# Column attention's row sums: four column tiles at once, in two runs of four products, each behind one half's scores of a later group

## The reference, cut to what matters

```python
scores = jnp.einsum('neax,nebx->neab', Q * scale, K)      # each sequence as 16 heads x 256 x 8
A = jax.nn.softmax(scores, axis=2)                        # over a, not over b
Out = jnp.einsum('neab,neax->neax', A, V)                 # V weighted by the row sums of A
```

## Time and profile before

| what | value |
|---|---|
| median of 3 executions | 1783.86 us (1780.13 to 1784.83) |
| the profiled execution, its own time | 1789.27 us |
| its span in the profile | 1787.5 us |
| PE busy | 1688.6 us (94%) |
| DVE busy | 1340.3 us (75%) |
| ACT busy | 1307.9 us (73%) |
| POOL busy | 1124.5 us (63%) |
| loop of the column attention | from 847.7 us to 1106.9 us of the span |

### The profile page before, as it was taken

The page is one execution under the profiler, slowest core; times in us unless marked ns, Lnnn a source line. Parts: engine busy times, 40 slices in busy tenths (PEclk is TensorE's granted clock), DMA queues, the critical chain, the costliest instruction groups (busy, mean ns, idle before and its releaser), DMA issues. The chain is left out here.

```text
span 1787.5 us, 43489 instructions
## 1 busy us (share of the span) xinstructions
PE 1688.6 (94%) x15560; PEld 1096.2 (61%) x15560; DVE 1340.3 (75%) x2367; ACT 1307.9 (73%) x4472; POOL 1124.5 (63%) x1014
## 2 busy tenths in 40 slices
PE   8997899999989999998999999899999999999999
PEld 5663677775657777554344444477776556777655
DVE  5554898974778989456688886698985688898645
ACT  5444788887358888745899998688887537888863
POOL 6554899992579999603212220799996278999730
PEclk9999999999999999999799999999999999999999
DMA  2002111103011110202655551211102102110111
GB/s 69 2 2 62 25 32 25 26 20 86 13 41 29 29 26 20 63 1 40 125 93 107 87 95 34 68 28 31 26 19 55 51 1 55 26 31 20 43 30 42
DMA packets 67309, 74.90 MB, mean 42 GB/s; under 512 B 13380, under 2 KB 50968, under 8 KB 65048
## 3 DMA queue, kind: packets, MB, share of 16 engines
q1 hardware_dynamic: 67096, 72.13, 18.9%
HBM read 28.08 MB, written 10.49 MB: 22 GB/s over the span
## 5 line engine op out<-in xcount | busy, mean ns | idle before, releaser
L457 POOL TENSOR_TENSOR rsum<-pa,pb 128x512 f32<-128x512 f32 x256 | 325.7, 1294 | 67.1 <-DVE pa L373 37.7
L839 ACT ACTIVATE ffn_prob<-sc,ffn_nmax 128x128 f32<-128x128 f32 x928 | 327.5, 387 | 6.8 <-DVE ffn_nmax L756 6.8
L923 POOL TENSOR_TENSOR ffn_prob<-ffn_prob,ffn_rden 128x512 f32<-128x512 f32 x256 | 265.7, 1060 | 54.3 <-DVE ffn_rden L771 46.7
L466 POOL TENSOR_TENSOR rsum<-rsum,ffn_rnt 128x512 f32<-128x512 f32 x256 | 262.0, 1045 | 8.2 <-ACT ffn_rnt L861 5.9
L383 DVE TENSOR_TENSOR pb<-proj,ffn_tab 128x512 f32<-128x512 f32 x236 | 161.5, 685 | 84.4 <-ACT rn L427 84.1
L839 ACT ACTIVATION_READ_ACCUMULATOR ffn_prob<-sc,ffn_nmax 128x1 f32 x928 | 209.5, 226 | 0.0
L363 PE MATMUL pt<-ident,rsum 128*128 128x128 f32 x960 | 154.2, 284 | 15.1 <-POOL rsum L466 12.4
L756 DVE TENSOR_REDUCE ffn_nmax<-sc 128x4 f32<-128x512 f32 x232 | 148.5, 682 | 16.1 <-PE sc L653 13.4
L363 PEld LDWEIGHTS pt<-ident,rsum 128*128 128x128 f32 x960 | 100.8, 141 | 96.6 <-ACT ffn_ptb L847 70.5
L394 DVE TENSOR_REDUCE ffn_ss<-rn 128x16 f32<-128x1024 f32 x128 | 154.4, 1206 | 0.0
L682 PE MATMUL ob<-ffn_ptb,ffn_v 128*64 128x64 f32 (+1 forms) x3072 | 143.7, 243 | 9.1 <-issue 9.1
(11 more groups left out here) (291 smaller groups left out, 4275.7 us busy)
## 6 DMA issues: line engine op xcount, KB each, us to landing
ffn_v<-ffn_v SPq DMA_DIRECT2D x128, 128.0 KB, 2.3
column_ks<-qk_parts SPq DMA_DIRECT2D x64, 128.0 KB, 4.1
rn<-Y SPq DMA_DIRECT2D x32, 128.0 KB, 2.3
qk_parts<-column_hi SPq DMA_DIRECT2D x64, 64.0 KB, 1.6
qk_parts<-column_lo SPq DMA_DIRECT2D x64, 64.0 KB, 1.7
column_qs<-qk_parts SPq DMA_DIRECT2D x32, 128.0 KB
column_qs<-qk_parts SPq DMA_DIRECT2D x64, 64.0 KB
rn<-Y SPq DMA_DIRECT2D x32, 127.5 KB, 2.4
```

The costliest lines, as they stand in the source:

```text
L457: pool.tensor_tensor(K.sm[:, r, w], K.m1[:, r, w], K.m2[:, r, w], ALU.add).then_inc(S.f_sum, 1)
L466: pool.tensor_tensor(heads(K.sm[:, r, w]), heads(K.sm[:, r, w]), K.rnt[:, r, w * HEADS:(w + 1) * HEADS].unsqueeze(2).broadcast_to([P, HEAD ...
L839: ins = act.activation(K.prob[:, r, e, k], score_banks(i)[e][:, tokens(k)], ACT.Exp, bias=K.nmax[:, r, e, k:k + 1], accum_out=K.den[:, r, ...
L923: pool.tensor_tensor(K.prob[:, r, e], K.prob[:, r, e], K.rden[:, r, e].unsqueeze(2).broadcast_to([P, 4, P]), ALU.mult).then_inc(S.f_pn, 1)
```

## The change

In the column attention PE's `row_sums` takes as its last argument bt in place of the half: one run has four products for the four tiles c = 0 to 3 with the same bt. A run with bt = 0 stands behind `scores(., 1)` of the next group, the one with bt = 1 behind `scores(., 0)` of the group after that. All waits on b_rs and b_rd count whole groups now. The product of a projection moves ahead of `scores(., 1)`. The finish of a sequence moves back: take, widen, weigh on DVE to groups 1, 2, 3 of the next sequence and residual to group 0 of the one after it; turn and spread on PE to groups 2 and 3, project to group 0 of the sequence after. After the loop PE has one more run of row sums and a `project` ahead of the last two runs, DVE a `residual`. In the local attention two of ACT's copies change places at tiles 27 and 28.

```diff
 (local attention, ACT)
-            if 1 <= i <= LATE:
+            if 1 <= i <= LATE + 1:
                 keep_probabilities(i - 1)
             if 0 <= i < TILES:
                 exponentials(i)
             if LATE + 1 < i < TILES:
                 keep_output(i - 2)
-            if LATE < i <= TILES:
+            if LATE + 1 < i <= TILES:
                 keep_probabilities(i - 1)
...
-            if 1 <= i <= LATE:
+            if 1 <= i < LATE:
                 keep_output(i - 1)
             if 0 <= j - 1 < TILES:
                 keep_queries(act, K, n, j - 1, pt[0])
+            if i == LATE:
+                keep_output(i - 1)
 (column attention, PE)
-            def row_sums(q, G, h):
+            def row_sums(q, G, bt):
...
-                pe.wait_ge(S.b_rd, 8 * q + 2 * G + h + 1)
+                pe.wait_ge(S.b_rd, 8 * q + 2 * G + 2)
...
-                for bt in range(2):
-                    for c in B_HALVES[h]:
-                        mm = pe.matmul(row_banks[q % 2][32 * c:32 * c + 4, 0:SEQ], B.rd[:, G, c, bt], B.E[:, 4 * (G % 2) + c, bt],
-                                       start=(G == 0 and bt == 0), stop=(G == 3 and bt == 1))
+                for c in range(4):
+                    mm = pe.matmul(row_banks[q % 2][32 * c:32 * c + 4, 0:SEQ], B.rd[:, G, c, bt], B.E[:, 4 * (G % 2) + c, bt],
+                                   start=(G == 0 and bt == 0), stop=(G == 3 and bt == 1))
...
-                    before = (q, G - 1) if G else (q - 1, 3)
+                    step = 4 * q + G
                     scores(q, G, 0)
-                    if before[0] >= 0:
-                        row_sums(*before, 0)
-                    scores(q, G, 1)
+                    if step >= 2:
+                        row_sums(*divmod(step - 2, 4), 1)
                     g = (q + 3) // 2
                     if 1 <= g < PAIRS:
                         if q % 2 and G <= 1:
                             product(g, G)
                         if q % 2 == 0 and G == 0:
                             product(g, 2)
-                    if q >= 1 and G >= 1:
-                        (turn, spread, project)[G - 1](q - 1)
-                    if before[0] >= 0:
-                        row_sums(*before, 1)
+                    scores(q, G, 1)
+                    if step >= 1:
+                        row_sums(*divmod(step - 1, 4), 0)
+                    if q >= 2 and G == 0:
+                        project(q - 2)
+                    if q >= 1 and G >= 2:
+                        (turn, spread)[G - 2](q - 1)
+            row_sums(SEQS - 1, 2, 1)
+            project(SEQS - 2)
             row_sums(SEQS - 1, 3, 0)
 (column attention, DVE)
-                    dve.wait_ge(S.b_rs, 8 * (q - 1) + 2 * G + h + 1)
+                    dve.wait_ge(S.b_rs, 8 * (q - 1) + 2 * G + 2)
...
-                    if q >= 1:
-                        (take, widen, weigh, residual)[G](q - 1)
+                    if q >= 2 and G == 0:
+                        residual(q - 2)
+                    if q >= 1 and G >= 1:
+                        (take, widen, weigh)[G - 1](q - 1)
...
+            residual(SEQS - 2)
             take(SEQS - 1)
 (column attention, ACT)
-                                act.wait_ge(S.b_rs, 8 * q + 2 * G + h - 3)
+                                act.wait_ge(S.b_rs, 8 * q + 2 * G - 2)
```

More of the change, by code:

```diff
@@ L1776, in scores @@
                     mm.then_inc(S.b_sc, 1)
-            def row_sums(q, G, h):
-                if q == 0 and G == 0 and h == 0:
+            def row_sums(q, G, bt):
+                if q == 0 and G == 0 and bt == 0:
                     pe.wait_ge(S.b_zero, 2)
-                pe.wait_ge(S.b_rd, 8 * q + 2 * G + h + 1)
-                if G == 0 and h == 0 and q >= 2:
+                pe.wait_ge(S.b_rd, 8 * q + 2 * G + 2)
+                if G == 0 and bt == 0 and q >= 2:
                     pe.wait_ge(S.b_rc, q - 1)
-                for bt in range(2):
-                    for c in B_HALVES[h]:
-                        mm = pe.matmul(row_banks[q % 2][32 * c:32 * c + 4, 0:SEQ], B.rd[:, G, c, bt], B.E[:, 4 * (G % 2) + c, bt],
-                                       start=(G == 0 and bt == 0), stop=(G == 3 and bt == 1))
+                for c in range(4):
+                    mm = pe.matmul(row_banks[q % 2][32 * c:32 * c + 4, 0:SEQ], B.rd[:, G, c, bt], B.E[:, 4 * (G % 2) + c, bt],
+                                   start=(G == 0 and bt == 0), stop=(G == 3 and bt == 1))
                 mm.then_inc(S.b_rs, 1)
```

## The result

The changed kernel takes 1801.99 us (median of 4, 1798.28 to 1808.2) against 1782.17 us of the kernel before (4 runs, 1780.13 to 1784.83): a ratio of 1.0114, 95% interval 1.0094 to 1.0135. It is slower, by 1.1%, where 1766 us was forecast. The range, 1757 to 1776, does not hold it, and the way it went had a chance of 0.04.

The account below looks back on a forecast made before the run. ACT was taken to bound the column attention, with gaps in it; savings of 11.8 + 1.2 + 2.7 + 2.0 - 0.1 = 17.6 us against the median of 1783.86 gave 1766 us, range 1757 to 1776.

Parts of the forecast that it names:

- the clock rival: Column attention: thinner PE work lowers the clock to 1.2 GHz and makes the kernel slower; 1810 with ten such sequences; chance 0.04.
- The rival's price: Column attention at 1.2 GHz: some 4.4 us more per sequence than forecast; 1810 with ten low sequences; chance 0.04.
- The run of row sums: PE in the column attention: a run of four products takes 0.53 us instead of 0.97.
- Group 0: Column attention, sequences 2 to 12: a gap of 0.4 us ahead of the next group's exponentials instead of 0.78.
- Group 1: Column attention, odd sequences: a gap of 0.25 us, with `take` in place of `residual`.
- Groups 2 and 3: Column attention, no projection there: both gaps (0.51 and its like in odd sequences) go, with 0.1 to spare.
- `take`: DVE in the column attention: `take` runs without idle time before it, where it had waited 0.82 us.
- `weigh`: DVE in group 3: needs `spread`, about 5.95, takes 0.33; maximum at 6.4, exponential at 7.1 us.
- Sequence 1: Column attention's low-clock stretch: groups 0 and 1 take 10.8 us instead of 13.49, 2.7 us saved.
- The local attention: Copy swaps at tiles 27 and 28, four times: PE's scores come 0.47 us earlier, 2.0 us saved (0 to 4).
- The new wait on a row sum: Rival: exponentials wait for a just-issued run; half of 56 groups lose 0.3, 8 us back, 1774; chance 0.16.

Follow-up runs that it names:

- the kernel with `project` first: Changed kernel with `project` ahead of the second scores, projection behind them, four-tile runs only in some groups from sequence 2 on: 1766.65 us, 0.9917 to the kernel before.
- the old order with wide runs: Kernel before with both row-sum runs four column tiles wide, one behind the other: 1809.69 us, ratio 1.0148.
- the kernel with the early two tiles: Changed kernel with two-tile row-sum runs in sequences 0 and 1 only, no added work: 1804.63 us, 1.0105 to the kernel before.
- full filler, start in two tiles: Changed kernel plus three unread full-array products in groups without projection from sequence 2, two-tile runs in sequences 0 and 1: 1769.01 us, 0.9919 to the kernel before.
- the wide filler: Changed kernel plus three times four unread products of 4 weight columns in groups without projection from sequence 2: 1775.61 us, 0.9950 to the kernel before.

## Why the prediction was wrong

**The step that failed** is the weight against the clock rival: "there PE had been idle for over half, here in no group by more than a third". I read the one fall in the loop before as a matter of idle time, and weighed the new thinness in that unit. The idle time was near the forecast (a quarter of a group; 0.67 of 3.40 us ahead of the fall at 961.3) and is not what decides by itself. The changed kernel fell behind stretches with TensorE busy for 2.73 of 3.40 us and the kernel with `project` first behind 3.00, while the kernel before held the full clock over stretches with 2.57, and the old order with wide runs shows both behind 2.58. What the runs showed in its place: with one and the same order, the width of the runs of row sums makes the difference, eight records in 0.97 us before, eight in 0.55 now. With the runs two tiles wide the changed kernel is at a granted clock of 1.00 from 890 to 1075 us; with four it is at 0.72 from 883 to 1081. The earlier trace rows already held a warning that I noted and set aside: 13.6 us at 1.2 GHz with TensorE busy for 13.06 of them.

That the clock is the cause is shown from three sides: the same order with two-tile runs holds it (0.9995), four-tile runs in the old order lose it (1.0148), and the changed kernel with work added in its thin groups and a start in two tiles lies in the forecast's range (1769.01 us).

**The rival's price** came near the total (1810 against 1801.99) by luck, as its parts were off. It said some 4.4 us more for a sequence at the low level, where its own groups (5.4 with a projection, 4.3 without) give 3.5 for an even and 4.3 for an odd one; sequences that are low throughout, in the kernel with the early two tiles, take 19.57 (sequence 4) and 20.88 (sequence 5), which is 4.7 and 5.8 more than forecast. And instead of ten whole sequences, parts of nearly all were low: from sequence 4 to 12 groups 1 to 3 of even and 2 and 3 of odd ones, 17.15 and 16.98 us a sequence where 14.85 and 15.1 were forecast.

**The run of row sums**, 0.53 forecast, is 0.55. The rows of the linear attention were the right ones.

**Group 0**, a gap of 0.4: with the clock held (full filler, start in two tiles) it is 0.52 in even sequences and 0.58 in odd ones. **Group 1**, 0.25: 0.16. **Groups 2 and 3**, none: none. The chain through the projection, the maxima, `residual` and `keep` is what stands ahead of the maximum, and the kernel with `project` first shows it from the other side: with the projection behind the scores the gap is 0.27.

**`take`** no longer waits in group 0, as forecast; `weigh`, with 0.1 to spare in my sum, is the one that the low clock turned into a wait of 1.82.

**Sequence 1**, 2.7 saved: not so. The clock was low from 841.8 to 882.8 us in the changed kernel, and sequences 0 to 3 lost 5.7 us instead.

**The local attention**, 2.0: 0.6, and 1.6 of a low stretch that did not come again in the second one. The first scores moved as forecast, and nearly all of it was lost again at once: the other swap, counted as free, puts the copy of the probabilities ahead of the exponentials of tile 28, and that copy waits 0.29 for PE.

**The new wait on a row sum** appeared only with runs of 0.97, in the kernel with two tiles, where it costs 0.68 into group 0.

The Trainium skill (TensorE: Matmul & The Clock Gate, section "Why this matters for your kernels") names idle gaps between bursts of matmuls as what makes the throughput drop. By that rule the changed kernel is safe: in the stretch ahead of the fall at 961.3 us TensorE idles for 0.67 us in all. The measurement differs from the rule, and decides. The Trainium skill (TensorE: Matmul & The Clock Gate, section "Loop structure matters more than you think") says that the loop nest determines whether matmuls stay at the full clock. With this the runs agree for the innermost loop alone: 1.0114 and 0.9995 differ in which products share a run and in nothing else, while the order of the larger pieces, new (1.0114) or old (1.0148), did not keep the clock up.

**What stays open.** Why a low stretch ends when it does: with nearly the same instructions it lasted 88.7 us in one kernel and 6.8 or 10.2 in each sequence later in it. And what exactly the clock follows: the runs show that it is not TensorE's busy time alone, and that runs four tiles wide let it fall where runs two tiles wide did not, not by what measure. Whether narrow products hold it less well than full ones stays open too: the wide filler let it fall four times from sequence 2 on and the full filler with the start in two tiles once, but the wide one takes TensorE for 0.10 us less each time.

## What to carry to other kernels

Where TensorE is nearly full and another engine is the bound, making TensorE's work denser can lower its clock and lose more than it saves (here 1.1% slower, where 1% was to be saved). Look for groups that would be thin, and make only those products dense that something waits for: that kernel needed no added work, kept a granted clock of 1.00 and was 0.7% faster than before. Read the row of the granted clock before any busy share: a TensorE that is busy throughout at 0.50 does not look idle.

## What was unexpected in the hardware

- The clock fell behind stretches with TensorE busy for 2.73 and 3.00 of 3.40 us, and did not behind 2.57 of 3.40 where the row sums took two column tiles instead of four.
- At 1.2 GHz TensorE was busy for 88.03 of 88.70 us and stayed there.
- At the same TensorE time, 2.58 of 3.40 us, the clock fell behind one stretch of the old order with wide runs and did not behind another.
- 0.86 us of unread products in most groups, with two-tile runs at the start, made the changed kernel 33 us faster (1801.99 to 1769.01 us, in different comparisons; the ratios to before are 1.0114 and 0.9919).
